# Experts in 27 tiles of 256 rows instead of 19 of 384, with two of eight low halves of the weights formed by VectorE

## The reference

```python
logits = xf @ router_w + router_b                  # xf: 3008 x 256, 4 experts
probs = softmax(logits); top_p, top_i = top_k(probs, 2)
gates = top_p / sum(top_p), put at top_i
h = silu(xf @ w1[e]) * (xf @ w3[e])                # per expert: 256 -> 1024, twice
out = sum over e of gates[:, e] * (h @ w2[e])      # 1024 -> 256
```

## Time and profile before

| | us |
|---|---|
| median of 3 runs | 1986.19 (1984.2 to 1987.22) |
| the profiled execution's own time | 1976.96 |
| its span | 1975.2 |
| of the span: from the first `up` to the last `down` | 1012.7 to 1537.0 |
| PE busy over the span | 1598.1 (81%) |
| DVE, ACT, POOL busy | 1215.2, 1019.2, 1113.8 |

### The profile page before, as it was taken

How to read it: one execution, slowest core, us unless ns; L and a number is a source line. 1 busy time by engine, 2 the same in 40 slices (tenths; PEclk the granted TensorE clock), 3 DMA queues, 4 the chain that set the end, 5 groups by cost and what they waited for, 6 DMA issues and landing times. The chain is left out here.

```text
span 1975.2 us, 32428 instructions
## 1 busy us (share of the span) xinstructions
PE 1598.1 (81%) x11205; PEld 1482.6 (75%) x11205; DVE 1215.2 (62%) x2392; ACT 1019.2 (52%) x2231; POOL 1113.8 (56%) x859
## 2 busy tenths in 40 slices
PE   7749999999999999997559999999999144698219
PEld 4338898989898989886459999999999134587219
DVE  6756575757575756574625666666555255458886
ACT  3536474746464756563435555555555123359452
POOL 0487675758575758561746767676777253207500
PEclk9869998999999999996569999999999566799659
DMA  4162000000000000001355555555565300003123
GB/s 186 63 203 83 1 8 0 8 0 8 8 0 8 0 8 0 8 1 49 130 168 166 144 137 141 142 144 137 142 152 144 73 16 24 24 1 118 42 91 110
DMA packets 74344, 142.59 MB, mean 72 GB/s; under 512 B 7400, under 2 KB 50472, under 8 KB 73736
## 3 DMA queue, kind: packets, MB, share of 16 engines
q1 hardware_dynamic: 63736, 127.54, 20.7%
q0 software_dynamic: 10512, 13.83, 4.2%
HBM read 107.89 MB, written 46.57 MB: 78 GB/s over the span
## 5 line engine op out<-in xcount | busy, mean ns | idle before, releaser
L1463 POOL TENSOR_TENSOR expert_w_low<-expert_raw,expert_w_high 128x768 fp32r<-128x768 f32 x152 | 289.5, 1959 | 155.2 <-ACT expert_w_high L1322 154.3
L646 ACT ACTIVATE probs<-psum,neg_max 120x376 f32<-120x376 f32 (+2 forms) x384 | 176.4, 479 | 140.0 <-DVE neg_max L763 140.0
L716 POOL TENSOR_TENSOR qk_low<-rotated,qk_high 128x376 fp32r<-128x376 f32 x128 | 138.4, 1081 | 180.2 <-ACT qk_high L639 175.8
L533 PE MATMUL psum<-diag,probs 128*128 128x128 f32 (+2 forms) x1536 | 203.5, 283 | 26.9 <-DVE pt_low L779 22.7
L533 PEld LDWEIGHTS psum<-diag,probs 128*128 128x128 f32 (+2 forms) x1536 | 185.6, 194 | 36.3 <-issue 25.6
L779 DVE TENSOR_TENSOR pt_low<-psum,pt_high 128x752 fp32r<-128x752 f32 x128 | 120.5, 941 | 142.6 <-ACT pt_high L655 141.6
L1439 DVE TENSOR_TENSOR expert_act_low<-expert_act,expert_act_high 128x384 fp32r<-128x384 f32 x152 | 148.6, 978 | 79.6 <-ACT expert_act_high L1360 79.6
L1360 ACT ACTIVATE expert_act_high<-expert_act 128x384 fp32r<-128x384 f32 x152 | 79.8, 525 | 171.3 <-DVE expert_act L1434 171.3
L1281 PE MATMUL psum<-slots_high,expert_w_high 128*128 128x384 f32 x608 | 158.2, 341 | 8.8 <-DVE expert_act L1434 7.6
L1281 PE MATMUL psum<-slots_low,expert_w_high 128*128 128x384 f32 x608 | 155.2, 336 | 0.0
L1281 PE MATMUL psum<-slots_high,expert_w_low 128*128 128x384 f32 x608 | 155.2, 336 | 0.0
(11 more groups left out here) (304 smaller groups left out, 4624.6 us busy)
## 6 DMA issues: line engine op xcount, KB each, us to landing
expert_raw<-in_experts SPq DMA_DIRECT2D x152, 384.0 KB, 3.1
x_slots<-in_c_slots SPq DMA_DIRECT2D x4, 3168.0 KB, 28.4
slot_rows<-x_slots SPq DMA_DIRECT2D x19, 396.0 KB, 4.6
up_spill<-held SPq DMA_DIRECT2D x5, 1128.0 KB, 5.0
held<-up_spill SPq DMA_DIRECT2D x5, 1128.0 KB, 5.8
patch<-in_patches SPq DMA_DIRECT2D x4, 752.0 KB, 6.8
hid_spill<-hid SPq DMA_DIRECT2D x1, 3008.0 KB, 8.5
resid<-hid_spill SPq DMA_DIRECT2D x8, 376.0 KB, 3.5
```

The costliest lines, as they stand in the source:

```text
L533: last = pe.matmul(psum[0:nj, BANK_PT + bank, at:at + ni], probs[0:ni, h % 2, src:src + nj], diag[0:ni, h % 2, it, 0:ni], start=True, stop ...
L646: last = act.activation(probs[0:ni, h % 2, at:at + P * it + ni], score_bank(h % 2, it), ACT.Exp, bias=neg_max[0:ni, h % 2, it:it + 1], acc ...
L716: pool.tensor_tensor(qk[1][:, c % 2, k, :], rotated[:, k, :], qk[0][:, c % 2, k, :].bitcast(F32), ALU.subtract).then_inc(qk_ready, 1)
L1463: pool.tensor_tensor(w[1][:, g % RING, :], raw[:, g % RAW, :], w[0][:, g % RING, :].bitcast(F32), ALU.subtract).then_inc(w_low, 1)
```

## The change

A tile becomes 256 rows (2 blocks of 128) instead of 384 (3 blocks). With the same formula there are 27 tiles. All widths of 384 in the stage become 256, except those of the weights (768) and of the quantised groups (384), and each tile has one block and one add less: the adds stand at f = 2 and 4. The eight chunks of weights are still loaded and split anew for each tile, 216 chunks in place of 152. Of the eight low halves of a tile's weights, VectorE now forms those of chunks 3 and 7, and GpSimd the other six. A wait that was on the count of all low halves is now on the one or the other count, by the chunk.

```diff
-TILE_SLOTS = 384
+TILE_SLOTS = 256
...
+        ON_DVE = (3, 7)
+        low_by_dve = sem("expert_low_by_dve")
...
+        def wait_low(engine, g):
+
+            if g % CHUNKS in ON_DVE:
+                engine.wait_ge(low_by_dve, split_on_dve(g))
+            else:
+                engine.wait_ge(w_low, g + 1 - split_on_dve(g))
...
                         if g >= RAW:
-                            sp.wait_ge(w_low, g - RAW + 1)
+                            wait_low(sp, g - RAW)
...
-                    pe.wait_ge(w_low, g + 1)
+                    wait_low(pe, g)
...
+                def split_low(g):
+                    dve.wait_ge(w_high, g + 1)
+                    dve.tensor_tensor(w[1][:, g % RING, :], raw[:, g % RAW, :], w[0][:, g % RING, :].bitcast(F32),
+                                      ALU.subtract).then_inc(low_by_dve, 1)
...
                     dve.tensor_tensor(act_hl[1][:, g % 2, :], act_f[:, g % 2, :], act_hl[0][:, g % 2, :].bitcast(F32),
                                       ALU.subtract).then_inc(low_made, 1)
+                    if g + AHEAD < last_chunk and (g + AHEAD) % CHUNKS in ON_DVE:
+                        split_low(g + AHEAD)
...
                 for g in range(last_chunk):
                     i, f = g // CHUNKS, g % CHUNKS
-                    if g + AHEAD < last_chunk:
+                    if g + AHEAD < last_chunk and (g + AHEAD) % CHUNKS not in ON_DVE:
                         split_low(g + AHEAD)
```

More of the change, by code:

```diff
@@ L1220, in expert_tiles, with split_on_dve @@
         AHEAD, TURN_AT, TURNED_AT, KEEP_AT, GATE_AT, LOAD_AT, ADD_AT = 4, (2, 4), (3, 5), 1, 2, 6, (2, 4, 6)[:BLOCKS]
+        ON_DVE = (3, 7)
+        low_by_dve = sem("expert_low_by_dve")
+        def split_on_dve(g):
+            return sum(i % CHUNKS in ON_DVE for i in range(g + 1))
+        def wait_low(engine, g):
[3 more added lines that the diff above has]
+                engine.wait_ge(w_low, g + 1 - split_on_dve(g))
         with nc.Block() as block:
@@ L1425, in round_weights @@
                     dve.tensor_tensor(split(n), split(n), per_block(wscale[:, u, :, :]), ALU.mult).then_inc(wq_made, 1)
+                def split_low(g):
+                    dve.wait_ge(w_high, g + 1)
+                    dve.tensor_tensor(w[1][:, g % RING, :], raw[:, g % RAW, :], w[0][:, g % RING, :].bitcast(F32),
+                                      ALU.subtract).then_inc(low_by_dve, 1)
                 keep_low(0, 0)
                 keep_low(0, 1)
+                for g in range(AHEAD):
+                    if g % CHUNKS in ON_DVE:
+                        split_low(g)
                 for g in range(last_chunk):
@@ L1475, in _ @@
                 for g in range(AHEAD):
-                    split_low(g)
+                    if g % CHUNKS not in ON_DVE:
+                        split_low(g)
                 for g in range(last_chunk):
                     i, f = g // CHUNKS, g % CHUNKS
-                    if g + AHEAD < last_chunk:
+                    if g + AHEAD < last_chunk and (g + AHEAD) % CHUNKS not in ON_DVE:
                         split_low(g + AHEAD)
```

## The result

The changed kernel takes 2104.64 us (median of 4 runs, 2104.53 to 2107.31) against 1986.49 of the kernel before: a ratio of 1.06, with an interval of 1.0582 to 1.0618. That is 118 us slower. The forecast was 2084 with a range of 2005 to 2115, and slower at 0.85.

What follows compares the result with a forecast made beforehand. The ring of ScalarE and VectorE, with VectorE waiting for GpSimd at SBUF, was to replace TensorE as bound: 15 x 21.3 + 12 x 25.6 = 626.7 us, +102.4 - 4.6, giving 2074.8, plus 9.2 to the median: 2084, range 2005 to 2115.

Steps and rivals of the forecast that it cites:

- the ring: ScalarE and VectorE handing each chunk to each other; expected to bound the changed kernel in place of TensorE.
- the second rival: TensorE stays the bound, tiles 17.5 plus 0.4 for the wait on keep_out: 1962 us, faster; chance 0.13.
- The bare ring: One chunk's handing over between ScalarE and VectorE without other waits: 1.93 us, against TensorE's 2.14.
- The pair of splits: Late in a tile, VectorE's low half of f = 7 waits for two back-to-back GpSimd splits: 1.78 us more.
- The gates: At f = 2, three small VectorE instructions: 0.36 us, 0.45 with the low half in front waiting for GpSimd.
- The turn: TensorE's turning of the next rows, ready at 8.3 where ScalarE would take them at 7.8: 0.5 us.
- VectorE's split at f = 3: VectorE's new low half of weights: 0.94 us itself, delaying the product of f = 4 by 1.16.
- f = 5 to 6: Step with a low half at f = 5 behind GpSimd's split: 0.26 us added to the ring.
- Group tiles: Tiles that also measure (f = 3) and round (f = 6) a weight group: 25.6 us, 4.3 over a plain tile.
- Sum: 15 x 21.3 + 12 x 25.6 = 626.7 us for the stage, +102.4; one add less at the end, -4.6.
- The ring without the port: First rival: GpSimd's paired splits cost VectorE nothing; plain tiles 19.2, group tiles 22.7, 2018 us; chance 0.19.
- The clock's: Third rival: TensorE's clock also falls after its waits in group tiles, 24 us more: 2108; chance 0.10.

Runs made afterwards that it cites:

- Experiment 7: Changed kernel with product in PSUM, gates at f = 7, GpSimd's adds at f = 3 and 7, VectorE's splits a chunk later: 1981.07 us.
- Experiment 5: Changed kernel with VectorE's three gate instructions at f = 7 in place of f = 2: 2095.54 us, ratio 1.0549.
- second profile of before: A further profile of the kernel before, unchanged: 1983.77 us.
- experiment 4: Changed kernel with GpSimd's low halves after the first eight chunks covering only 32 of 768 columns, most of that computation left out: 2003.83 us, ratio 1.0091.

## Why the prediction was right, and where its sizes were off

- **What bounds.** Right: TensorE gives way to the ring. Busy 0.83 (0.8 predicted), and ScalarE's waits for the product (L1455) the longest of all. Among TensorE's own waits those for the low half (58.7 us) come before those for the product (37.4), other than the signs of the prediction had it. Experiment 7 shows the floor that I gave TensorE in the second rival, 17.9 a plain tile, to the tenth.
- **The bare ring**, 1.93 a chunk. Right: silu to silu is 1.92 in the plain tile above (1601.28 to 1603.20), product to product 1.90 from f = 4 to f = 5.
- **The pair of splits.** The mechanism was right, the place was not. I had the low half of f = 6 slip in with 0.4 us to spare and that of f = 7 blocked; in the trace that of f = 6 is blocked for 4.17. From the product of f = 6 to the first of the next tile it is 7.51 us (1601.69 to 1609.20), in place of 2 x 1.93 + 2.52 = 6.38: +1.13 a tile.
- **The gates** at f = 2. This is the term that was mis-sized most: 0.45 expected for all three, after the 0.16 of the earlier trace rows, and 1.81 in the trace for the first alone. I took an instruction of 8 columns as too small to matter, but it has two inputs in SBUF and stands behind a low half that has just let GpSimd's next split go ahead. Product 2 to 3: 3.76 in place of 2.4, +1.36.
- **The turn and VectorE's split at f = 3.** The 0.5 of the wait for the turn did not come, since the gates had already held the ring up: 3.12 for 3.87, -0.75. Experiment 5 takes the gates away and the wait returns. The split itself is 0.96 (0.94 predicted, bounds 0.56 and 1.12).
- **f = 5 to 6**: 2.19 in place of 2.47, -0.28. The sum is 1.36 - 0.75 - 0.28 + 1.13 = 1.46 of plain tile; measured 22.65 - 21.3 = 1.35. Over 15 tiles 20 us, which is the size of the miss. That it is no larger is in part luck: two terms too small by 2.5 us a tile were met by two too large by 1.0.
- **Group tiles** 26.1 for 25.6, but only 3.45 over the plain one in place of 4.3: measuring was not blocked (0.54, 0.17 and 0.23), and the rounding follows right behind the blocked pair, as said. 12 x 0.5 = 6 more.
- **Sum.** 20.3 + 6 of tiles, less some 4 at the stage's ends, come on top of the +102.4: 125.2 measured. The tail gave 7.5 for 4.6 (5.2 against the second profile of before). Together 117.7 for 97.8, and so 2104.6 for 2084.
- **The rivals.** The ring without the port was no bad sum: 19.2 and 22.7 a tile, and experiment 4, which takes the port's cause away, has 18.9 and 21.9. It only wasn't this kernel. The clock's was not this kernel either. The granted clock did fall, to 0.50 for some 3 us behind TensorE's wait at f = 6 and 7, and in plain tiles too. Of the twelve whole plain tiles eight had 0.92 or 0.93 on the mean and four had 1.00, as the one above. The eight took 22.64 to 22.77 us, the four 22.60 to 22.66: 0.06 us a tile on the mean. TensorE was busy for 538 us of the stage with what takes it 495 in experiment 7, and the ring hid the difference. A stretch at the low clock, and the tile behind the one above:

```profile
1585.00:1588.00 3.00, 3.00 (x16) 3.00 (x15) 2.08 (x4) 1.91 (x4) 0.00 (x0) 0.50 0.83 232
1611.44:1634.10 22.66, 18.52 (x138) 18.14 (x139) 16.74 (x25) 12.30 (x27) 14.20 (x9) 0.92 0.65 166
```

The Trainium skill, "TensorE: Matmul & The Clock Gate", section "HAM oscillation — how this bites in real kernels", has waits between bursts bring the clock down. The group tile (0.93) and the eight plain ones agree; the tile from 1588.84, at 1.00 with its gap of 2.47 us, shows that not each wait does.

What stays open: why VectorE gets in between two splits of GpSimd at one place and waits for both at another. In the changed kernel all 25 low halves that waited for both met a second split whose high half had been ready for 0.66 us or more when the first split ended; of those that got in after one, none met a second split that had been ready for more than 0.03. No run varied that by itself.

## What to carry to other kernels

A smaller tile lowers the bound of the engine that is full and leaves all per-tile work of the others as it is: before making it smaller, lay out one tile of the next bound with all that stands beside its chunks, for that slack was what hid it. Count every VectorE instruction with two inputs in SBUF as able to wait for GpSimd, however small, and move one input to PSUM or GpSimd's work elsewhere before moving work between the two. And what comes back when one wait is taken out of a ring is set by what is late next, not by the wait: 1.85 us gave 0.37 a tile at the gates, while four edits together took away all of it.

## What the runs showed of the hardware

- A VectorE instruction of 8 columns with two inputs in SBUF took 1.81 us beside a GpSimd split and 0.15 to 0.16 without one. One of 256 columns took 4.17 beside two back to back, 1.00 where it got in between, and 0.42 to 0.43 with one input in PSUM, always.
- The rounding step that adds and subtracts a constant (L1437) has one input and took 1.88 us (at 1265.45 in experiment 7) in place of 0.43: right beside GpSimd's splits it waited as well. So one input in SBUF is no promise for every instruction. No run varied this one by itself.
- Writing the product to PSUM in place of SBUF cost VectorE nothing: 429 ns for 421 on the mean.
- The 768-column difference that costs GpSimd 1.84 takes VectorE 0.96, 2.19 where it waited for GpSimd.
- Two profiles of the kernel before begin the experts 10.0 us apart (the whole spans are 6.8 apart). The later one has six waits at one line of the router, 13.2 us in all and up to 5.1, that end with no releaser in the trace. What they are is open.
- The granted clock at 0.50 for some 3 us cost a plain tile, which the ring bounds, 0.06 us of 22.65.
